# Seven products for eight in the gate and up projections of a fused attention and FFN layer, with down weights loaded at the end

## The chip, the cores and the metric

One Trainium2 chip, all 8 cores, each running the same program on other data. The metric is the time of one execution in device microseconds, which is that of the slowest core. On every core TensorE (PE) does the matrix products, VectorE (DVE), ScalarE (ACT) and GpSimd (POOL) work on elements, and SyncE (SP), ACT and POOL issue DMA transfers.

## What is computed

For four sequences of 4096 tokens of width 1024:

```
s = LN(x) W_spin^T + b;  g = mean(s) W_global;  e = s W_J
x1 = x + LN(tanh(beta * (s + g + softmax(e s^T / 32) s)))
y  = LN(x1);  gate = y w_gate^T / 127;  up = y w_up^T / 127
out = x1 + LN((silu(gate) * up) w_down^T / 127)
```

The hidden width is 3072. The three FFN weights come as int32 between -127 and 127.

## The kernel before

Core c holds sequence c // 2. It projects all 4096 tokens of it, and does the rest for its own 2048 tokens: 16 tiles of 128, or 4 blocks of 512. Matmul operands are bf16, and each matmul is 128x128 by 128x512 into one of the 8 banks of PSUM (`ps`). Each engine has a program of its own (`pe_prog`, `act_prog`, `vec_prog`, `pool_prog`, `sync_prog`), written in the order in which it runs, and waits on semaphores by hand. The stages are:

1. `PHASE_A` (L403 to L448): s and e.
2. `scores` and `values` (L450 to L498) for the 16 token tiles, with softmax, tanh and both layer norms on DVE and ACT. SP transposes each normalised tile `xn2` by DMA into `xn2T` (L292).
3. Gate and up (L500 to L520). The hidden dimension has 24 tiles of 128 (`HC`). A unit is one hidden tile by one block of 512 tokens: 8 matmuls over the 8 slices of the width for gate (L510) and 8 for up (L517). `UNITS` (L45) lists the 96 units. Gate goes to bank n % 4, up to bank 4 + n % 4, so a bank comes round every fourth unit. ACT turns the gate bank into silu in `silu_b` (L620), and DVE multiplies it by the up bank into `h_act` (`h_mul`, L835 to L843).
4. Down (L522 to L543). For each token tile, 24 matmuls into each of two banks, then the last layer norm and the residual: DVE L887 to L914, ACT L628 to L640. SP loads the rows of x1 again (`x1_load`, L296), the first four of them when the last unit is done.

POOL issues the weight loads (L363 to L389). They turn int32 into bf16 on the way, 256 KB landed per tile of gate or of up. The down weights come as six loads of 1 MB (L387) between those of gate and up, and TensorE waits for all six at L522. At the start of stage 3 DVE still has the layer norms of the last token tile to do, so the first products of `h_mul` stand between them:

```python
            h_mul(0)
            ln2_stats(u)
            h_mul(1)
            ln2_apply(u)
            for n in range(2, N_UNIT):
                h_mul(n)
```

## Time and profile before

| What | Value |
|---|---|
| median of 3 runs | 1144.13 us (1143.34 to 1144.13) |
| the profiled execution, its time | 1143.46 us |
| its span on the slowest core, core 2 | 1141.9 us (other cores 1140.5 to 1141.8) |
| TensorE busy | 1116.8 us, 98%, 5200 matmuls |
| DVE, ACT, POOL busy | 446.7, 260.2 and 97.4 us |
| granted TensorE clock | 0.999 on all cores |
| gate and up / down on TensorE | 637.5 to 969.0 us / 969.0 to 1134.8 us |

The span runs from the first to the last instruction of a core; the time of the execution is 1.56 us longer. Times in rows are microseconds from the start of the span unless marked ns. "PEld" is TensorE loading weights, and L510 is line 510 of the kernel.

### The profile page before, as it was taken

What the parts mean: (1) busy time and instruction counts of PE and PEld (TensorE: products, weight loads), DVE (VectorE), ACT (ScalarE), POOL (GpSimd) and SP (SyncE); (2) the same over time, 40 slices, a digit from 0 to 9 for tenths busy, and PEclk for the clock granted to TensorE, in tenths of its full rate; (3) what the DMA queues carried; (4) which work ended last, traced back from release to release, by engine and by line L of the source; (5) the groups of instructions that cost most, each with busy time, mean ns of one, the idle gap of its engine ahead of it and who ended that gap; (6) DMA issues with size and microseconds to landing.
All of it is one profiled execution on the core that took longest, in us unless ns stands there. A gap on an engine that the chain in (4) does not pass through costs nothing.

```text
span 1141.9 us, 15173 instructions; the slowest of 8 cores (1140.5 to 1141.9 us)
## 1 busy us (share of the span) xinstructions
PE 1116.8 (98%) x5200; PEld 508.2 (45%) x5200; DVE 446.7 (39%) x1145; ACT 260.2 (23%) x458; POOL 97.4 (9%) x130
## 2 busy tenths in 40 slices
PE   3999999999999999999999999999999999999997
PEld 2444444444444444444444444444444444444443
DVE  5277600345555555555555721211121122233233
ACT  4434443312222222222222111111111111111111
POOL 4000001001111111111111111111110000000000
PEclk9999999999999999999999999999999999999999
DMA  9988798624433434343333534445542220432321
GB/s 201 205 183 208 165 180 158 106 53 88 89 88 88 86 84 97 94 90 88 90 85 84 105 62 75 74 74 74 74 75 38 37 38 1 148 94 92 111 92 55
DMA packets 172219, 112.15 MB, mean 98 GB/s; under 512 B 146416, under 2 KB 148464, under 8 KB 172144
## 3 DMA queue, kind: packets, MB, share of 16 engines
q1 hardware_dynamic: 151680, 64.77, 25.1%
q0 software_dynamic: 19168, 41.95, 19.7%
q10 hardware_dynamic: 1296, 4.46, 1.2%
q8 instruction: 43, 0.70, 0.3%
q14 instruction: 32, 0.26, 0.1%
HBM read 83.89 MB, written 16.78 MB: 88 GB/s over the span
## 4 chain that ended last, share of the span: by engine, by line
PE 97%; DMA 1%; DVE 0%; issue 0%; ACT 0%; ACTq 0%; DVEq 0%
PE ps L480 19%; PE ps L461 19%; PE ps L510 15%; PE ps L539 15%; PE ps L517 15%; PE ps L445 13%; PE ps L432 2%; DMA xs<-x 1%; PE ps L491 0%; PE ps L396 0%; DVE st L690 0%; ACT xnT L556 0%; ACTq L548 0%; DVE st L691 0%; ACT ob L636 0%
## 5 line engine op out<-in xcount | busy, mean ns | idle before, releaser
L461 PE MATMUL ps<-s_FM,eT 128*128 128x512 bf16 x1024 | 223.6, 379 | 0.0
L480 PE MATMUL ps<-s_tok,pT 128*128 128x512 bf16 x1024 | 223.5, 379 | 0.0
L517 PE MATMUL ps<-xn2T,wgu 128*128 128x512 bf16 x768 | 181.4, 379 | 0.0
L510 PE MATMUL ps<-xn2T,wgu 128*128 128x512 bf16 x768 | 181.4, 379 | 0.0
L539 PE MATMUL ps<-wdT_sb,h_act 128*128 128x512 bf16 x768 | 165.9, 379 | 0.0
L839 DVE SCALAR_TENSOR_TENSOR h_act<-silu_b,ps 128x512 bf16<-128x512 f32 x96 | 65.9, 687 | 251.0 <-PE ps L517 250.5
L480 PEld LDWEIGHTS ps<-s_tok,pT 128*128 128x128 bf16 x1024 | 100.3, 98 | 120.7
L461 PEld LDWEIGHTS ps<-s_FM,eT 128*128 128x128 bf16 x1024 | 100.1, 98 | 120.9
L607 ACT ACTIVATE S_sb<-S_sb,nmx 128x1024 bf16<-128x1024 f32 x64 | 72.7, 1136 | 215.8 <-DVE nmx L773 215.8
L620 ACT ACTIVATE silu_b<-ps 128x512 f32<-128x512 f32 x96 | 57.2, 597 | 268.5 <-PE ps L510 257.8
L539 PEld LDWEIGHTS ps<-wdT_sb,h_act 128*128 128x128 bf16 x768 | 75.1, 98 | 90.6
L517 PEld LDWEIGHTS ps<-xn2T,wgu 128*128 128x128 bf16 x768 | 75.1, 98 | 90.6
L510 PEld LDWEIGHTS ps<-xn2T,wgu 128*128 128x128 bf16 x768 | 75.1, 98 | 90.7 <-issue 0.3
L764 DVE TENSOR_SCALAR_CACHE_REDUCE S_sb<-ps 128x1024 f32<-128x1024 f32 x64 | 78.3, 1223 | 71.5 <-PE ps L461 67.8
L445 PE MATMUL ps<-xnT,wspT_sb 128*128 128x512 bf16 x448 | 97.3, 379 | 0.0
L445 PEld LDWEIGHTS ps<-xnT,wspT_sb 128*128 128x128 bf16 x448 | 43.8, 98 | 52.9
L586 ACT ACTIVATE s_FM<-ps,b_col_sb 128x512 bf16<-128x512 f32 x64 | 43.8, 687 | 58.3 <-PE ps L445 51.0
L791 DVE SCALAR_TENSOR_TENSOR sg<-ps,rinv,sg 128x1024 f32<-128x1024 f32 x16 | 20.5, 1283 | 80.8 <-PE ps L480 80.8
L445 PE MATMUL ps<-s_FM,wjT_sb 128*128 128x512 bf16 x224 | 48.8, 379 | 0.0
L357 POOL TENSOR_TENSOR sg<-s_tok,g_bc 128x1024 f32<-128x1024 bf16 x16 | 34.2, 2134 | 169.0 <-ACT a_bf L602 141.0
L602 ACT ACTIVATE a_bf<-sg,beta_sb 128x1024 bf16<-128x1024 f32 x16 | 18.4, 1147 | 123.9 <-DVE sg L791 123.9
L889 DVE BATCH_NORM_STATS2 st<-ps 128x6 f32<-128x512 f32 x16 | 11.2, 699 | 71.7 <-PE ps L539 71.7
(82 smaller groups left out, 515.6 us busy)
## 6 DMA issues: line engine op xcount, KB each, us to landing
xs<-x SPq DMA_DIRECT2D x24, 512.0 KB, 5.8
xr<-x POOLq DMA_DIRECT2D x16, 512.0 KB, 5.4
x_sc<-xr POOLq DMA_DIRECT2D x16, 512.0 KB, 3.0
x1b<-x_sc SPq DMA_DIRECT2D x16, 512.0 KB, 3.8
out<-ob SPq DMA_DIRECT2D x15, 512.0 KB, 3.8
wgu<-wg POOLq DMA_DIRECT2D x24, 256.0 KB, 4.9
wgu<-wu POOLq DMA_DIRECT2D x24, 256.0 KB, 5.8
wdT_sb<-wdT POOLq DMA_DIRECT2D x6, 1024.0 KB, 12.5
```

Of the source, the lines that this page charges most:

```text
L357: gp.tensor_tensor(out=sg[:], in0=s_tok[:, t - 1, :], in1=g_bc[:], op=ALU.add).then_inc(l_sg, 1)
L445: mm = pe.matmul(bank(b0 + c), w[:, i, o:o + P], moving(i), start=(i == 0), stop=(i == KC - 1))
L461: mm = pe.matmul(bank(2 * slot + half), eT[:, j, t * P:(t + 1) * P], s_FM[:, j, m0:m0 + 512], start=(j == 0), stop=(j == KC - 1))
L480: mm = pe.matmul(bank(pv_bank(t) + nb), pT[:, m, :], s_tok[:, m, nb * 512:(nb + 1) * 512], start=(m == 0), stop=(m == NT - 1))
L510: mm = pe.matmul(bank(n % 4), wgu[:, hb % 3, 0, j, :], xn2T[:, j, tb * 512:(tb + 1) * 512], start=(j == 0), stop=(j == KC - 1))
L517: mm = pe.matmul(bank(4 + n % 4), wgu[:, hb % 3, 1, j, :], xn2T[:, j, tb * 512:(tb + 1) * 512], start=(j == 0), stop=(j == KC - 1))
L539: mm = pe.matmul(bank(2 * slot + nb), h_act[:, c, t * P:(t + 1) * P], wdT[:, c, nb * 512:(nb + 1) * 512], start=(c == 0), stop=(c == HC - 1))
L586: s.activation(out=s_FM[:, c, b * 512:(b + 1) * 512], in_=src, func=AF.Identity, bias=b_col[:, c:c + 1], scale=1.0, accum_out=racc[:, c * ...
L607: s.activation(out=p_view(q), in_=S_sb[:, q, :], func=AF.Exp, bias=nmx[:, t % 2:t % 2 + 1], scale=1.0, accum_out=rs[:, 4 * (t % 2) + q: 4 ...
L620: s.activation(out=silu_b[:, n % 2, :], in_=bank(n % 4), func=AF.Silu).then_inc(a_silu, 1)
L764: v.tensor_scalar(out=S_sb[:, q, :], in0=bank2(2 * (n % 3)), scalar1=INV32, scalar2=None, op0=ALU.mult, op1=ALU.max, accum_out=mx[:, 4 * ( ...
L839: v.scalar_tensor_tensor(out=h_act[:, hb, tb * 512:(tb + 1) * 512], in0=silu_b[:, n % 2, :], scalar=INV127, in1=bank(4 + n % 4), op0=ALU.m ...
```

## The change

**Gate and up.** The first pair of hidden tiles is done as before, in 8 units; of the four token blocks, each is now done for both tiles in turn. The other 11 pairs are done by Strassen's scheme. A step is one pair by two blocks (`STEPS`, 22 of them; q is 0 for token blocks 0 and 1, 1 for blocks 2 and 3). For gate the weights form a 2x2 matrix A (rows: the two hidden tiles, columns: the two halves of the width), and the tokens a matrix B (rows: halves of the width, columns: the two blocks). The plain product needs eight products of such parts for gate, each of 4 matmuls, and Strassen's needs seven, M1 to M7; up is the same. That is 56 matmuls in a step where there were 64. `PRODUCTS` is their order: (m, 0) is product m of gate, (m, 1) of up.

**Sums of inputs.** B11+B22, B11+B12 and B21+B22 go to `u_x`, and B21-B11 and B12-B22 take the place of B21 and B12 in `xn2T`: five DVE additions (`x_sum`) of 128x2048 bf16 for each half of the tokens, between and after the `h_mul` of the first pair. For each pair of weights POOL makes A11+A22, A12-A22 and A21-A11 (`weight_sum`), and DVE -(A21+A22) and -(A11+A12) (`weight_sums`), each 128x1024 bf16 and each for gate and up together.

**Sums of outputs.** A step has two banks for gate and two for up, here z and w. M1 is made in z, and ACT copies it to w, from PSUM to PSUM (L808, L819). M4, -M5 and M7 are then added in z, M3, -M2 and M6 in w, and the banks end as C11 and C22. On the way ACT copies M1, M1+M4 and M1+M3 to SBUF (`t_m1`, `t_14`, `t_13`); POOL makes M4 and M1+M3+M4 of them (L493, L498); and DVE subtracts the bank from that, before M7 and M6 may be added: C12 in `t_14`, C21 in `t_13` (L1157, L1162). ACT takes silu of the four gate blocks, DVE multiplies by up (`hidden`). Steps alternate between two sets of four banks.

**Down weights.** Each of the 24 hidden tiles has its own tile `wdT[c]` and its own load of 256 KB. Six are issued in step (3, 1), seven at the start of step (11, 0), and the last eleven at the start of step (11, 1), the last one. Token tiles 0 and 1 of the down stage are done together, hidden tile by hidden tile, each waiting for its own load.

In the diff, `a_cp`, `a_sl` count ACT's copies and silus, `v_c`, `v_hs`, `v_u`, `v_ws` DVE's subtractions, hidden products and sums, `l_e`, `l_ws` POOL's, and `p_m` TensorE's products.

```diff
-UNITS = ([(0, 0), (0, 1), (0, 2), (1, 0), (1, 1), (1, 2), (0, 3), (1, 3)]
-         + [(hb, tb) for hb in range(2, HC) for tb in range(4)])
...
+UNITS = [(0, 0), (1, 0), (0, 1), (1, 1), (0, 2), (1, 2), (0, 3), (1, 3)]
...
+STEPS = [(p_, q_) for p_ in range(1, NPAIR) for q_ in range(2)]
...
+PRODUCTS = [(1, 0), (1, 1), (4, 0), (3, 0), (4, 1), (3, 1), (5, 0), (2, 0),
+            (5, 1), (2, 1), (7, 0), (6, 0), (7, 1), (6, 1)]
...
+        wd_home = ([192 + 2 * i for i in range(6)]
+                   + [56 + 2 * i for i in range(7)]
+                   + [2 * i for i in range(8)]
+                   + [32 + 2 * i for i in range(3)])
+        wdT = [at(f"wdT{c}", [P, D], BF16, wd_home[c] * KB)
+               for c in range(HC)]
+        WD_EARLY, WD_MID = 6, 13
...
+        def w_operand(s_, gu, m):
+            raw, ext = wraw[s_], wsum[s_]
+            return {1: ext[:, gu, 0, :], 2: ext[:, gu, 1, :],
+                    3: raw[:, gu, 0, 0:512], 4: raw[:, gu, 1, 512:1024],
+                    5: ext[:, gu, 2, :], 6: raw[:, gu, 1, 0:512],
+                    7: raw[:, gu, 0, 512:1024]}[m]
+        def x_operand(q, m):
+            xt, u = xn2T[q], u_x[q]
+            return {1: u[:, 0], 2: xt[:, 0:4, 0:512], 3: xt[:, 0:4, 512:1024],
+                    4: xt[:, 4:8, 0:512], 5: xt[:, 4:8, 512:1024],
+                    6: u[:, 1], 7: u[:, 2]}[m]
+        def step_bank(it, gu, w):
+            return 4 * (it % 2) + 2 * gu + w
...
+            def load_pair(p_):
+                s_ = p_ % 2
+                for i in range(2):
+                    for gu, w_d in enumerate((wg_d, wu_d)):
+                        gp.dma_start(
+                            out=wraw[s_][:, gu, i, :].rearrange(
+                                "p (k f) -> p k f", f=P),
+                            in_=w_d[2 * p_ + i]).then_inc(d_gu[s_][i], 16)
...
+            def weight_sum(p_, i):
+                s_ = p_ % 2
+                raw, ext = wraw[s_], wsum[s_]
+                a11, a12 = raw[:, :, 0, 0:512], raw[:, :, 0, 512:1024]
+                a21, a22 = raw[:, :, 1, 0:512], raw[:, :, 1, 512:1024]
+                if i == 0:
+                    for h in range(2):
+                        gp.wait_ge(d_gu[s_][h], 32 * (p_ // 2 + 1))
+                    gp.tensor_tensor(out=ext[:, :, 0, :], in0=a11, in1=a22,
+                                     op=ALU.add).then_inc(l_ws, 1)
+                    return
+                gp.wait_ge(v_ws, 2 * p_)
+                out, sub = ((a12, a22), (a21, a11))[i - 1]
+                gp.tensor_tensor(out=out, in0=out, in1=sub, op=ALU.subtract
+                                 ).then_inc(l_ws, 1)
...
+                if (p_, q) == (NPAIR - 1, 0):
+                    gp.wait_ge(p_m, NP * it)
+                    for c in range(WD_EARLY, WD_MID):
+                        load_wd(c)
+                if (p_, q) == (NPAIR - 1, 1):
+                    gp.wait_ge(p_m, NP * it)
+                    for c in range(WD_MID, HC):
+                        load_wd(c)
+                for gu in range(2):
+                    gp.wait_ge(a_cp, 8 * it + 5 + 2 * gu)
+                    gp.tensor_tensor(out=t_14[gu][:], in0=t_14[gu][:],
+                                     in1=t_m1[gu][:], op=ALU.subtract
+                                     ).then_inc(l_e, 1)
+                    gp.wait_ge(a_cp, 8 * it + 6 + 2 * gu)
+                    gp.wait_ge(l_e, 4 * it + 2 * gu + 1)
+                    gp.tensor_tensor(out=t_13[gu][:], in0=t_13[gu][:],
+                                     in1=t_14[gu][:], op=ALU.add
+                                     ).then_inc(l_e, 1)
+                if nxt < NPAIR and q == 0:
+                    weight_sum(nxt, 0)
+                elif nxt < NPAIR:
+                    weight_sum(nxt, 1)
+                    weight_sum(nxt, 2)
...
+            for it, (p_, q) in enumerate(STEPS):
+                s_ = p_ % 2
+                for m, gu in PRODUCTS:
+                    if m == 1 and gu == 0:
+                        for h in range(2):
...
+                    elif m == 4:
+                        pe.wait_ge(a_cp, 8 * it + 1 + 2 * gu)
+                    elif m == 3:
+                        pe.wait_ge(a_cp, 8 * it + 2 + 2 * gu)
+                    elif m == 5:
+                        pe.wait_ge(a_cp, 8 * it + 5 + 2 * gu)
+                        pe.wait_ge(v_ws, 2 * p_)
+                    elif m == 2:
+                        pe.wait_ge(a_cp, 8 * it + 6 + 2 * gu)
+                    elif m == 7:
+                        pe.wait_ge(v_c, 4 * it + 1 + 2 * gu)
+                        pe.wait_ge(l_ws, 3 * p_ - 1)
+                    else:
+                        pe.wait_ge(v_c, 4 * it + 2 + 2 * gu)
...
+            pe.wait_ge(v_h, N_UNIT)
+            pe.wait_ge(a_sl, 4 * (N_STEP - 1))
+            pe.wait_ge(v_hs, 4 * (N_STEP - 1))
+            for c in range(HC):
+                pe.wait_ge(d_wd[c], 16)
+                for t in range(2):
+                    for nb in range(2):
+                        mm = down(t, nb, c)
+                        if c == HC - 1:
+                            mm.then_inc(p_dn, 1)
+            for t in range(2, NQ):
+                if t == 2:
+                    pe.wait_ge(a_sl, 4 * N_STEP)
+                    pe.wait_ge(v_hs, 4 * N_STEP)
+                elif t >= 4:
...
+                n0 = 8 * it
+                zg, wg_, zu, wu_ = [bank(step_bank(it, gu, w))
+                                    for gu in range(2) for w in range(2)]
+                s.wait_ge(p_m, product_done(it, 1, 0))
+                if it == 1:
+                    s.wait_ge(v_h, N_UNIT)
+                s.copy(out=wg_, in_=zg).then_inc(a_cp, 1)
+                s.wait_ge(a_cp, n0 + 1)
+                if it == 0:
+                    s.wait_ge(v_h, N_UNIT)
+                else:
+                    s.wait_ge(v_hs, 4 * it - 1)
+                s.copy(out=t_m1[0][:], in_=wg_).then_inc(a_cp, 1)
+                s.wait_ge(p_m, product_done(it, 1, 1))
+                if it >= 2:
+                    s.wait_ge(v_hs, 4 * (it - 1))
+                s.copy(out=wu_, in_=zu).then_inc(a_cp, 1)
+                s.wait_ge(a_cp, n0 + 3)
+                if it >= 1:
+                    s.wait_ge(v_hs, 4 * it)
+                s.copy(out=t_m1[1][:], in_=wu_).then_inc(a_cp, 1)
+                for gu, (z, w) in enumerate(((zg, wg_), (zu, wu_))):
+                    s.wait_ge(p_m, product_done(it, 4, gu))
+                    s.copy(out=t_14[gu][:], in_=z).then_inc(a_cp, 1)
+                    s.wait_ge(p_m, product_done(it, 3, gu))
+                    s.copy(out=t_13[gu][:], in_=w).then_inc(a_cp, 1)
+                for i, t_ in enumerate((t_14[0], t_13[0])):
+                    s.wait_ge(v_c, 4 * it + i + 1)
+                    s.activation(out=t_[:], in_=t_[:], func=AF.Silu
+                                 ).then_inc(a_sl, 1)
+                for i, (t_, z, m) in enumerate(((t_m1[0], zg, 7),
+                                                (t_m1[1], wg_, 6))):
+                    s.wait_ge(p_m, product_done(it, m, 0))
+                    s.wait_ge(l_e, 4 * it + 2 * i + 1)
+                    s.activation(out=t_[:], in_=z, func=AF.Silu
...
+                b11, b12 = xt[:, 0:4, 0:512], xt[:, 0:4, 512:1024]
+                b21, b22 = xt[:, 4:8, 0:512], xt[:, 4:8, 512:1024]
+                v.wait_ge(d_xn2T, 16 * (8 * q + 8))
+                if i >= 3:
+                    v.wait_ge(p_up, 4 * q + 4)
+                out, in0, in1, op = ((u_[:, 0], b11, b22, ALU.add),
+                                     (u_[:, 1], b11, b12, ALU.add),
+                                     (u_[:, 2], b21, b22, ALU.add),
+                                     (b21, b21, b11, ALU.subtract),
+                                     (b12, b12, b22, ALU.subtract))[i]
+                v.tensor_tensor(out=out, in0=in0, in1=in1, op=op
+                                ).then_inc(v_u, 1)
+            def weight_sums(p_):
+                s_ = p_ % 2
+                for h in range(2):
+                    v.wait_ge(d_gu[s_][h], 32 * (p_ // 2 + 1))
+                for i, h in ((1, 1), (2, 0)):
+                    v.scalar_tensor_tensor(
+                        out=wsum[s_][:, :, i, :],
+                        in0=wraw[s_][:, :, h, 0:512], scalar=-1.0,
+                        in1=wraw[s_][:, :, h, 512:1024],
+                        op0=ALU.mult, op1=ALU.subtract).then_inc(v_ws, 1)
+            v.wait_ge(p_qk, 4 * NQ)
+            h_mul(2)
+            x_sum(0, 0)
+            h_mul(3)
+            x_sum(0, 1)
+            h_mul(4)
+            x_sum(0, 2)
+            weight_sums(1)
+            h_mul(5)
+            x_sum(0, 3)
+            h_mul(6)
+            x_sum(0, 4)
+            h_mul(7)
+            v.wait_ge(v_u, 5)
+            for i in range(5):
+                x_sum(1, i)
...
+            for it, (p_, q) in enumerate(STEPS):
+                for gu in range(2):
+                    v.wait_ge(l_e, 4 * it + 2 * gu + 2)
+                    v.wait_ge(p_m, product_done(it, 5, gu))
+                    v.tensor_tensor(out=t_14[gu][:], in0=t_13[gu][:],
+                                    in1=bank(step_bank(it, gu, 0)),
+                                    op=ALU.subtract).then_inc(v_c, 1)
+                    v.wait_ge(p_m, product_done(it, 2, gu))
+                    v.wait_ge(v_c, 4 * it + 2 * gu + 1)
+                    v.tensor_tensor(out=t_13[gu][:], in0=t_13[gu][:],
+                                    in1=bank(step_bank(it, gu, 1)),
+                                    op=ALU.subtract).then_inc(v_c, 1)
+                v.wait_ge(v_c, 4 * it + 4)
+                v.wait_ge(a_sl, 4 * it + 1)
+                hidden(it, 0, 1, t_14[0][:], t_14[1][:])
+                v.wait_ge(a_sl, 4 * it + 2)
+                hidden(it, 1, 0, t_13[0][:], t_13[1][:])
+                v.wait_ge(a_sl, 4 * it + 3)
+                v.wait_ge(p_m, product_done(it, 7, 1))
+                hidden(it, 0, 0, t_m1[0][:], bank(step_bank(it, 1, 0)))
+                v.wait_ge(a_sl, 4 * it + 4)
+                v.wait_ge(p_m, product_done(it, 6, 1))
+                hidden(it, 1, 1, t_m1[1][:], bank(step_bank(it, 1, 1)))
+                if q == 0 and p_ + 1 < NPAIR:
+                    weight_sums(p_ + 1)
```

What it moves, first on TensorE in the gate and up stage. Before, parts of two units (gate L510, up L517):

```order
L517 MATMUL ps<-xn2T,wgu 128x512 x7
L510 MATMUL ps<-xn2T,wgu 128x512 [waits d_gu1,d_xn2T,a_silu]
L510 MATMUL ps<-xn2T,wgu 128x512 x7
L517 MATMUL ps<-xn2T,wgu 128x512 [waits v_h]
L517 MATMUL ps<-xn2T,wgu 128x512 x7
```

Now, the start of step (2, 0) (`wsum` and `wraw` hold weights, `u_x` and `xn2T` tokens; M1 of gate, M1 of up, M4 of gate):

```order
L682 MATMUL ps<-u_x_66,wsum_70 128x512 [waits d_gu0_0,d_gu0_1,l_ws,a_sl]
L682 MATMUL ps<-u_x_66,wsum_70 128x512 x3
L682 MATMUL ps<-u_x_66,wsum_70 128x512 [waits v_hs]
L682 MATMUL ps<-u_x_66,wsum_70 128x512 x3
L686 MATMUL ps<-xn2T_45,wraw_68 128x512 [waits a_cp]
L686 MATMUL ps<-xn2T_45,wraw_68 128x512 x3
```

A wait now stands before every fourth matmul, and M4 of gate (the fifth row) waits for a copy that ACT makes of M1 of gate, with one product in between. M3 of gate, M4 and M3 of up follow with such waits too.

Next DVE, from the last layer norm on (`xn` is `xn2`). Before:

```order
L680 SCALAR_TENSOR_TENSOR nw<-nw 128x1 [waits v_seq]
L830 TENSOR_SCALAR xn_62<-xr,mv,nw 128x1024 [waits v_seq,d_xn2T]
L839 SCALAR_TENSOR_TENSOR h_act<-silu_b,ps 128x512 [waits a_silu,p_up] x94
L887 BN_STATS st_73<-ps 128x6 [waits p_dn]
L889 BN_STATS st_73<-ps 128x6 [waits p_dn]
```

Now, to the fourth addition over the first half of the tokens:

```order
L1056 SCALAR_TENSOR_TENSOR h_act<-tmp_72,ps 128x512 [waits p_qk,a_silu,p_up]
L1112 TENSOR_TENSOR u_x_66<-xn2T_45 128x2048 [waits d_xn2T]
L1056 SCALAR_TENSOR_TENSOR h_act<-tmp_73,ps 128x512 [waits a_silu,p_up]
L1112 TENSOR_TENSOR u_x_66<-xn2T_45 128x2048 [waits d_xn2T]
L1056 SCALAR_TENSOR_TENSOR h_act<-tmp_72,ps 128x512 [waits a_silu,p_up]
L1112 TENSOR_TENSOR u_x_66<-xn2T_45 128x2048 [waits d_xn2T]
L1121 SCALAR_TENSOR_TENSOR wsum_71<-wraw_69 128x2x512 [waits d_gu1_0,d_gu1_1]
L1121 SCALAR_TENSOR_TENSOR wsum_71<-wraw_69 128x2x512
L1056 SCALAR_TENSOR_TENSOR h_act<-tmp_73,ps 128x512 [waits a_silu,p_up]
L1112 TENSOR_TENSOR xn2T_45<-xn2T_45 128x4x512 [waits d_xn2T,p_up]
```

Between the products of the first pair stand the sums, here 128x2048 and 128x1024 in size; one more of the first half and five of the second follow.

Last POOL, near the end of its program. Before, at the last of the six loads of down weights:

```order
L381 DMA wgu<-wg 128x1024 [waits p_up]
L383 DMA wgu<-wu 128x1024
L387 DMA wdT_sb<-wdT 128x4x1024
L381 DMA wgu<-wg 128x1024 [waits p_up]
L383 DMA wgu<-wu 128x1024
```

Now, from the seventh load of step (11, 0) into the eleven of step (11, 1):

```order
L422 DMA wdT12_96<-wdT 128x1024
L493 TENSOR_TENSOR tmp2_74<-tmp2_74,tmp0_72 128x512 [waits a_cp]
L498 TENSOR_TENSOR tmp4_76<-tmp4_76,tmp2_74 128x512 [waits a_cp,l_e]
L493 TENSOR_TENSOR tmp3_75<-tmp3_75,tmp1_73 128x512 [waits a_cp]
L498 TENSOR_TENSOR tmp5_77<-tmp5_77,tmp3_75 128x512 [waits a_cp,l_e]
L422 DMA wdT13_97<-wdT 128x1024 [waits p_m]
L422 DMA wdT14_98<-wdT 128x1024
```

The additions that the banks wait for (L493, L498) now stand behind weight loads on the queue of POOL. The load of wdT6 to wdT12 comes ahead of the first row, that of the other ten of the last step behind the last.

## Rows read from the trace of the kernel before

**Rows 1.** The page: engines' busy time; all cores; shares of the chain.
```profile
PE 1116.8 (98%) x5200; PEld 508.2 (45%) x5200; DVE 446.7 (39%) x1145; ACT 260.2 (23%) x458; POOL 97.4 (9%) x130
...
PE 97%; DMA 1%; DVE 0%; issue 0%; ACT 0%; ACTq 0%; DVEq 0%
...
core 2: 1141.9 us, clock 0.999
```

**Rows 2.** Stretches: length, busy us (instructions) of PE, PEld, DVE, ACT, POOL, clock, DMA share, GB/s.
```profile
0.00:30.00 30.00, 11.84 (x82) 7.62 (x83) 16.26 (x45) 14.99 (x22) 12.55 (x24) 1.00 0.94 198
...
637.48:969.04 331.56, 331.56 (x1538) 150.21 (x1537) 75.99 (x132) 59.63 (x98) 27.36 (x49) 1.00 0.38 60
```

**Rows 3.** Groups by line: shapes and count, busy us, mean ns, idle before and its releasers.
```profile
L839 DVE SCALAR_TENSOR_TENSOR h_act<-silu_b,ps 128x512 bf16<-128x512 f32 x96 | 65.9, 687 | 251.0 <-PE ps L517 250.5 <-ACT silu_b L620 0.3 <-DVE mv L801 0.2
L620 ACT ACTIVATE silu_b<-ps 128x512 f32<-128x512 f32 x96 | 57.2, 597 | 268.5 <-PE ps L510 257.8 <-DVE h_act L839 10.7
L586 ACT ACTIVATE s_FM<-ps,b_col_sb 128x512 bf16<-128x512 f32 x64 | 43.8, 687 | 58.3 <-PE ps L445 51.0 <-PE ps L432 7.3
L357 POOL TENSOR_TENSOR sg<-s_tok,g_bc 128x1024 f32<-128x1024 bf16 x16 | 34.2, 2134 | 169.0 <-ACT a_bf L602 141.0 <-DVE g_bc L866 28.0
L812 DVE SCALAR_TENSOR_TENSOR xr<-a_bf,nw,xr 128x1024 f32<-128x1024 bf16 x16 | 20.6, 1285 | 2.9 <-DVE nw L680 2.9
L674 DVE TENSOR_TENSOR nw<-nw 128x1 f32<-128x1 f32 x96 | 15.3, 159 | 10.6 <-DVE nw L669 0.6 <-DVE nw L680 0.3
L754 DVE TENSOR_SCALAR mf_bc<-mf 128x1024 bf16<-128x1024 f32 x1 | 0.7, 693 | 0.1
L921 DVE TENSOR_TENSOR ob<-ob,x1b 128x512 f32<-128x512 f32 x1 | 0.7, 693 | 0.3 <-ACT ob L636 0.3
```

**Rows 4.** Timeline, the last unit of gate and up: start us, length us, instruction.
```profile
965.58 1.89 PE L510 MATMUL ps<-xn2T,wgu 128*128 128x512 bf16 x8
967.31 1.89 PE L517 MATMUL ps<-xn2T,wgu 128*128 128x512 bf16 x8
967.62 0.60 ACT L620 ACTIVATE silu_b<-ps 128x512 f32<-128x512 f32 x1 [2.86 <-PE ps L510]
969.04 21.32 PE L539 MATMUL ps<-wdT_sb,h_act 128*128 128x512 bf16 x98
969.31 0.69 DVE L839 SCALAR_TENSOR_TENSOR h_act<-silu_b,ps 128x512 bf16<-128x512 f32 x1 [2.77 <-PE ps L517]
```

**Rows 5.** Timeline, start of the kernel: DVE waits for itself, TensorE for ACT.
```profile
9.23 0.14 DVE L699 RECIPROCAL ri<-sd 128x1 f32<-128x1 f32 x1
...
9.48 0.16 DVE L701 SCALAR_TENSOR_TENSOR nb<-mv,ri 128x1 f32<-128x1 f32 x1
...
12.29 1.24 ACT L572 ACTIVATE xn<-xs,nb,ri 128x1024 bf16<-128x1024 f32 x1
...
13.64 0.78 PEld L396 LDWEIGHTS ps<-ident,xn 128*128 128x128 bf16 x8 [2.38 <-issue]
13.67 1.01 PE L396 MATMUL ps<-ident,xn 128*128 128x128 bf16 x8 [2.15 <-ACT xn L572]
```

**Rows 6.** Timeline of DVE, the end of the last layer norm.
```profile
654.02 0.81 DVE L830 TENSOR_SCALAR xn<-xr,mv,nw 128x1024 bf16<-128x1024 f32 x1 [0.18 <-DVE nw L680]
654.75 1.28 DVE L839 SCALAR_TENSOR_TENSOR h_act<-silu_b,ps 128x512 bf16<-128x512 f32 x2
```

**Rows 7.** Timeline of POOL: issues of one gate tile and of 1 MB of down weights.
```profile
721.11 0.53 POOL L381 DMA_DIRECT2D wgu<-wg  x1 [12.75 <-PE ps L517]
...
722.15 0.78 POOL L387 DMA_DIRECT2D wdT_sb<-wdT  x1
```

**Rows 8.** DMA from issue to landing: gate tile; down weights; x1b.
```profile
wgu<-wg POOLq DMA_DIRECT2D x24, 256.0 KB, 4.9
...
DMA to landing us min/median/max: 11.9/12.5/13.2
...
DMA to landing us min/median/max: 3.6/3.8/9.6
```

197 lines of the change are left out of this document (128 added, 69 removed).

## Prediction

> **What bounds the kernel now.** I read the page and the cores first. All cores end together at a granted clock of 1.00, the fuller of TensorE's two levels (2.4 GHz), and 97% of the chain that ended last is TensorE [rows 1]. So work taken off TensorE shortens the kernel, as far as nobody else becomes late. The stretches give TensorE's pace: gate and up last 331.56 us for 96 units of 16 matmuls (the row counts two at its edges besides), 215.9 ns each, busy all through [rows 2]. DVE is busy for 76 us of it, ACT for 60, POOL for 27. The groups give prices, and say that ACT and DVE spend their idle time there waiting for TensorE [rows 3]. What decides is how quickly results go round, so I read handoffs last, in timelines [rows 4, 5]. ACT starts 0.31 us after TensorE's next group has started (967.31 to 967.62), DVE 0.27 us after (969.04 to 969.31). From ACT's end (13.53) to TensorE's next matmul (13.67) it is 0.14 us. A DVE instruction that waits for DVE's last one starts 0.11 us behind its end (9.37 to 9.48); I take that for ACT, POOL and any pair of them too.
>
> **Removed from TensorE.** 22 steps x 8 matmuls = 176, at 215.9 ns: **-38.0 us**. 5024 are left. A product then lasts 4 x 0.2159 = 0.863 us, a step of 14 products 12.09 us. The pace itself stays: a wait that has been met costs nothing where the units have theirs (1536 matmuls fill the stage without a gap).
>
> **One step, followed through.** Times from its start, at which M1 of gate starts. M1 of gate is followed at 0.86, ACT starts its copy to bank w at 1.17, and ends at 1.77, with 0.60 as for L620 [rows 3]. M4 of gate can start at 1.91, and its place is 1.73: **0.18 us late**, in each of 22 steps, **+4.0 us**. No row shows ACT writing to PSUM. Below, I take 0.50 a copy (0.1 us less than any, 0.08 late, 1.8 us in all); above, the 0.687 of L586 (0.27 late, 5.9 us).
> The other copies have time: the second (1.88 to 2.48) frees M3 of gate, placed at 2.77 with the 0.18; the fifth, M1+M4 of gate, ends at 4.35, and M5 is placed at 5.36.
> POOL then adds four times, with one wait for itself in each pair. L357 takes 2.134 us for 1024 elements, so 1.07 for 512 [rows 3]. From 4.46: 5.53, then 5.64 to 6.71, to 7.78, and 7.89 to 8.96. DVE subtracts with 0.69 (L921): the third ends at 9.76, the fourth, which waits for it, at 10.56. M7 of up is placed at 10.54 and could start at 9.90; M6 of up at 11.40, and could at 10.70. So 0.64 us are spare in POOL's four additions: up to 1.23 us each they cost nothing. That is the narrowest cover of the change.
> In a step ACT has 12 x 0.6 = 7.2 us of work, DVE 8 x 0.69 and up to 2 x 1.29 of weight sums (L812), 8.1, POOL 4.3 and up to 4.3 of weight sums: all below 12.3. POOL's two sums of an odd step end at 8.96 + 2 x 2.13 + 0.11 = 13.3, 1.1 us into the next step; four loads at 0.53 [rows 7] end at 3.2, before it is needed at 4.46. Nothing on the path.
>
> **Start of the steps.** DVE's queue is behind here. Its last layer norm lets it go at 654.75 [rows 6], and TensorE needs the five sums of the first half after its 8 units, at 637.48 + 128 x 0.2159 = 665.11 [rows 2]. Before them stand five products at 0.64 and two weight sums at 1.285 (L812), 5.8 us. The price of a sum of 2048 bf16 elements is in no row. L754, the one DVE row with dense bf16 written and no second tensor, takes 0.693 us for 1024; less the 0.16 us of a single element (L674) this is 0.52 ns per element, 1.23 us for 2048. L921, TENSOR_TENSOR on 32-bit words, gives (0.693 - 0.16)/512 = 1.04 ns, 2.29 us. I take 1.23, because all three tensors are 16 bits wide here, as in L754's output. The sums end at 654.75 + 5.8 + 6.2 = 666.7, and the first step starts 1.7 us late: **+1.7 us**. The five sums of the second half end at 673.5, and M7 needs DVE at 674.5: hidden. With 2.29 the first step is 7.0 us late, DVE comes free 4.0 us late for M7, and the sum is 11.0 us.
> "VectorE: DVE Perf Modes" of the Trainium skill (section on the perf-mode tier table) has tensor_tensor on 2048 bf16 elements at 1224 ns, and 2293 ns on fp32; the second agrees with L921, the first is in no row.
>
> **Down weights.** In step (11, 0) POOL issues seven loads of 256 KB from 1.1 on: at 0.53 each, as a gate tile of the same size [rows 7], to 4.8, so its additions start 0.3 late, covered. In step (11, 1) eleven last from 0.1 to 6.0, its additions start 1.6 late, and 0.64 is spare: **+1.0 us**. At the 0.78 us of L387 it is 1.5 + 3.6 = 5.1 us, the upper end.
> Arrival: the gate tile issued at 721.11 lands after 4.9 us, at 726.0; the tile of up and the 1 MB behind it are in at 722.15 + 12.5 = 734.65 [rows 7, 8]. That is 1.25 MB in 8.65 us, 1.73 us for 256 KB. The eighteen late loads are then in at 1.1 + 4.9 + 17 x 1.73 = 35.4 from the start of (11, 0). The four x1b loads come among them and took up to 9.6 us [rows 8]: 45.0 at the latest. The last tile is needed at 2 x 12.27 + 1.0 + 92 x 0.2159 = 45.4. No cost, but only just: 10% less bandwidth makes 3 us. The wait for all six big loads at the stage's start (L522) had cost nothing, so nothing is gained. The first two token tiles end together, 20.7 us into the stage, but DVE has until the fifth tile, at 41 us.
>
> **Sum.** 1141.9 - 38.0 + 4.0 + 1.7 + 1.0 = 1110.6 us of span. The profiled execution took 1.56 us more than its span, and the median is 0.67 above that execution: **1112.8 us**. It is 2.7% below 1144.13.
>
> **Rivals.**
> *POOL and DVE get in each other's way.* In odd steps POOL's two weight sums run from 9.0 to 13.3, and DVE's first two hidden products (both factors in SBUF) are due at 10.7. If such a pair can't run together and POOL goes first, DVE starts at 13.3, and its third product, which frees `t_m1` for ACT's second copy, ends 3.1 us into the next step, not 0.8. The copy ends at 3.9, M3 starts at 4.0 instead of 2.8: 1.2 us in 10 steps, 12 us, **1125**. For it: no row has the two together, since L357 ran alone. Against: if DVE gets in between the two sums, it costs 0. 20%.
> "SBUF — State Buffer" of the Trainium skill (section Who interferes with whom) says that a DVE instruction with two SBUF inputs and a GpSimd instruction that reads SBUF can't run at once, and that the later one waits for the whole of the other. No row here shows it; by it alone this rival would be the forecast whenever POOL wins the second turn.
> *DVE's sums take 2.29 us.* +9.3 us, **1122**. 10%.
> *Down weights come too late.* 20% less bandwidth for casting loads beside x1b: 6 to 7 us at the start of down, **1119**. 8%.
> *Slower than before: POOL's additions of f32.* L357 reads one bf16 tensor; here both are 32 bits wide. If that doubles an element, an addition of 512 takes 2.13 us, each step is 4 x (2.13 - 1.23) = 3.6 us late at M7 of up, 22 times 79 us: **1192**. It decides from 1.23 us on, and the gain is gone at 1.23 + 33/88 = 1.6 us. Against: of L357's three tensors two, `g_bc` and `sg`, are 32 bits wide already. 4%.
> *The change doesn't do what it says.* The order of instructions shows the 176 matmuls gone, so it could only be that TensorE runs slower: if the gaps brought its granted clock down from 1.00, each percent over 22 steps would cost 2.7 us. At the kernel's start TensorE was busy for 11.84 of 30 us, and the granted clock was 1.00 [rows 2]. 3%, **1120**.
>
> **Chances.** The forecast as summed has 55%, the rivals 45%. The range from **1108 to 1130** takes in the lower ends (ACT at 0.50, sums hidden) and all rivals but the slow one, but not two of them together. A measurement of this kernel can tell 0.2%, some 2.3 us. Faster by more than that: 0.95, within it 0.01, slower 0.04.
>
> **What would show it.** Right: 5024 matmuls; M4 of gate idle before it by some 0.2 us for ACT L808, and nothing before M3, M5, M2; L493 and L498 near 1.07 us; one wait of 1 to 3 us before the first L682, released by DVE L1112 at 1.2 us each; one wait near 1 us for DVE at M7 of up in the last step; the down stage starting near 638 + 27.6 + 1.7 + 22 x 12.27 + 1 = 938. Wrong: TensorE waiting at M7 or M6 in every step (POOL's price), at M3 in even steps (the two in each other's way), at L693 for a weight load, or L808 longer than 0.7 us.

## The result and the profile after

The changed kernel takes **1136.68 us** (median; 1135.7 to 1137.2), the kernel before 1144.13: a ratio of 0.9936, 95% interval 0.9919 to 0.9953. It is faster, by 7.4 us, where a gain of 31.3 was forecast: 1112.8 us, with a range from 1108 to 1130. So 23.9 us have to be explained. Executions in which a die showed a markedly lower granted clock are left out of all ratios and ranges, here and below; they move the medians given by at most 0.4 us, and e7's, which they would move by 0.9, is given without them.

The profiled execution took 1136.68 us for a span of 1135.1 (core 5; the others 1129.8 to 1134.3, granted clocks 0.995 to 0.999). From the page, to set beside [rows 1]: busy times, the chain that ended last, and the down stage's matmuls (line, engine, tiles, count, busy us and mean ns, idle us before them).

```profile
PE 1089.2 (96%) x5024; PEld 487.4 (43%) x5024; DVE 570.8 (50%) x1265; ACT 357.2 (31%) x634; POOL 292.3 (26%) x269
...
PE 84%; issue 5%; POOL 4%; DVE 3%; ACT 2%; DMA 1%; POOLq 0%; ACTq 0%; DVEq 0%
...
L693 PE MATMUL ps<-wdT,h_act 128*128 128x512 bf16 x768 | 165.9, 379 | 0.0
```

The matmuls are gone, 5024 are left, and those of the down stage run without a gap. But TensorE's share of the chain fell from 97% to 84%, and POOL, DVE and ACT are in it. The waits of TensorE say where (what ended them; us in all, times, longest):

```profile
PE ps L686 <- ACT tmp L814: 9.8, 12, 0.9
PE ps L686 <- DVE tmp L1157: 7.1, 19, 1.5
...
PE ps L682 <- DVE xn2T L1112: 3.6, 1, 3.6
```

L814 is ACT's second copy, for which M3 of gate waits; L1157 the subtraction ahead of M7; L1112 the x sums. The rows are those of core 5, the slowest. The times at which M1 of gate starts (L682) give every step its length; the table has them for core 7, on which no weight load was late (more on that below). The forecast stands beside it:

| | forecast | core 7 |
|---|---|---|
| first step starts at | 666.8 | 668.59 |
| step 0 | 12.27 | 13.93 |
| the ten later steps with q = 0 | 12.27 | 13.6 each |
| the ten steps with q = 1, but the last | 12.27 | 12.4 each |
| the last step | 13.3 | 14.75 |
| down stage starts at | 938 | 957.63 |

On core 5 the down stage starts at 962.24. From there to the end it is 172.9 us on both cores, as in the kernel before (969.04 to 1141.9).

**The steps with q = 0.** Timeline of core 7 round the start of such a step, at 747.04 (start and duration in us, engine, line, tiles; in brackets idle time and what ended it):

```profile
744.16 4.66 POOL L439 TENSOR_TENSOR wraw<-wraw 128x1024 bf16<-128x1024 bf16 x2
...
746.03 3.34 DVE L1146 SCALAR_TENSOR_TENSOR h_act<-tmp,tmp 128x512 bf16<-128x512 f32 x2 [0.17 <-ACT tmp L837]
...
747.04 1.89 PE L682 MATMUL ps<-u_x,wsum 128*128 128x512 bf16 x8
...
749.29 1.27 DVE L1146 SCALAR_TENSOR_TENSOR h_act<-tmp,ps 128x512 bf16<-128x512 f32 x2
...
750.06 0.59 ACT L814 COPY tmp<-ps 128x512 f32<-128x512 f32 x1 [1.32 <-DVE h_act L1146]
...
750.79 2.75 PE L686 MATMUL ps<-xn2T,wraw 128*128 128x512 bf16 x12 [0.89 <-ACT tmp L814]
```

POOL makes the two weight sums of the step before, and beside them DVE's first two hidden products, both factors in SBUF, take 3.34 us, where such a pair takes 1.3 in the last step, with no sum of POOL's beside it. The same view in shorter windows parts the pairs:

```profile
746.25 2.57 POOL L439 TENSOR_TENSOR wraw<-wraw 128x1024 bf16<-128x1024 bf16 x1
...
746.76 2.60 DVE L1146 SCALAR_TENSOR_TENSOR h_act<-tmp,tmp 128x512 bf16<-128x512 f32 x1
```

POOL's first sum runs from 744.16 and takes 2.13 us, as if alone. DVE's first product starts at 746.03 and is over by 746.8; it came in between the two sums. POOL's second sum takes 2.57 us instead of 2.13, and DVE's second product, started inside it, 2.60 instead of 0.68. In the middle of that the new step starts. DVE's third product frees `t_m1` only then; ACT's copy had stood idle for 1.32 us, and M3 of gate for 0.89. TensorE waits so in ten steps.

The groups of core 7 (mean ns of one), to set beside [rows 3], between 600 and 960 us:

```profile
L493 POOL TENSOR_TENSOR tmp<-tmp,tmp 128x512 f32<-128x512 f32 x44 | 56.4, 1282 | 65.6 <-ACT tmp L826 65.6
L498 POOL TENSOR_TENSOR tmp<-tmp,tmp 128x512 f32<-128x512 f32 x44 | 55.8, 1267 | 6.3
L439 POOL TENSOR_TENSOR wraw<-wraw 128x1024 bf16<-128x1024 bf16 x22 | 51.7, 2373 | 11.6 <-DVE wsum L1121 11.6
L1146 DVE SCALAR_TENSOR_TENSOR h_act<-tmp,tmp 128x512 bf16<-128x512 f32 x44 | 50.1, 1177 | 3.8 <-ACT tmp L837 2.9 <-DVE tmp L1162 0.9
...
L1146 DVE SCALAR_TENSOR_TENSOR h_act<-tmp,ps 128x512 bf16<-128x512 f32 x44 | 28.0, 674 | 0.0
...
L1121 DVE SCALAR_TENSOR_TENSOR wsum<-wraw 128x1024 bf16<-128x1024 bf16 x22 | 25.8, 1211 | 0.0
L434 POOL TENSOR_TENSOR wsum<-wraw 128x1024 bf16<-128x1024 bf16 x11 | 23.4, 2126 | 0.0
...
L808 ACT COPY ps<-ps 128x512 f32<-128x512 f32 x22 | 12.6, 571 | 53.7 <-PE ps L682 53.7
```

POOL's additions take 1.27 us, not 1.07. A hidden product with a factor in PSUM takes 0.674 us, each time; one with both factors in SBUF 1.177 on the mean. ACT's copy to PSUM is quick, 0.571, and M4 of gate is 0.1 us late for it, where 0.18 was taken.

**The start of the steps.** The same view, and then windows of core 7 (the stretch, its length, PE busy and matmuls in it, the granted clock, DMA share, GB/s):

```profile
658.34 1.22 DVE L1112 TENSOR_TENSOR u_x<-xn2T 128x2048 bf16<-128x2048 bf16 x1
...
661.97 5.18 POOL L439 TENSOR_TENSOR wraw<-wraw 128x1024 bf16<-128x1024 bf16 x2 [11.62 <-DVE wsum L1121]
662.35 2.83 DVE L1112 TENSOR_TENSOR xn2T<-xn2T 128x2048 bf16<-128x2048 bf16 x1
...
665.70 2.54 DVE L1112 TENSOR_TENSOR xn2T<-xn2T 128x2048 bf16<-128x2048 bf16 x1
...
668.59 1.01 PE L682 MATMUL ps<-u_x,wsum 128*128 128x512 bf16 x2 [3.74 <-DVE xn2T L1112]
```

```profile
668.50:670.00 1.50, 1.41 (x4) 0.50 0.94 107
670.00:672.00 2.00, 2.00 (x7) 0.60 1.07 201
672.00:676.00 4.00, 4.00 (x20) 1.00 0.71 118
```

The first three x sums take 1.22 us each, as forecast. The last two meet POOL's L439 and take 2.83 and 2.54, and POOL's pair 5.18 instead of 4.3. TensorE stands still for 3.74 us. Then, which is in no term of the sum, the granted clock is 0.50 and 0.60: for most of these 3.5 us it is the lower of the two levels, 1.2 GHz. Eight matmuls last 3.36 us instead of 1.89. This does not follow on every core. On cores 1 and 3 the pause is as long (3.63 and 3.64 us), the granted clock stays at 1.00, and yet step 0 lasts 13.69 us, only 0.24 less than on core 7. So the lower clock is not what makes step 0 long. Core 1, the first matmuls and POOL's first two additions:

```profile
667.93 1.89 PE L682 MATMUL ps<-u_x,wsum 128*128 128x512 bf16 x8 [3.63 <-DVE xn2T L1112]
...
672.14 1.81 POOL L493 TENSOR_TENSOR tmp<-tmp,tmp 128x512 f32<-128x512 f32 x1 [3.42 <-ACT tmp L826]
...
674.09 2.06 POOL L498 TENSOR_TENSOR tmp<-tmp,tmp 128x512 f32<-128x512 f32 x1
```

The additions take 1.81 and 2.06 us instead of 1.27. DVE makes its last x sums of the second half beside them, until 675.0, and then waits 1.30 us for POOL (L498) before it can subtract; M7 of gate and of up are late in turn.

**The last step.** POOL on core 7:

```profile
943.60 5.87 POOL L422 DMA_DIRECT2D wdT<-wdT  x11 [3.56 <-PE ps L686]
949.39 1.37 POOL L493 TENSOR_TENSOR tmp<-tmp,tmp 128x512 f32<-128x512 f32 x1
...
953.53 1.26 POOL L498 TENSOR_TENSOR tmp<-tmp,tmp 128x512 f32<-128x512 f32 x1
```

The eleven issues end at 949.4, 6.5 us into the step. TensorE waits 1.50 us before M7 of gate and 0.74 before M7 of up.

### The profile page after: what moved, and what is told of

The parts are those of the page before. It is cut to its first block, busy times and chain, and to the rows that moved or that the text cites. A ratio compares the mean times of both kernels' runs of the same rounds, so it can differ in the third digit from the quotient of the medians.

```text
span 1135.1 us, 15989 instructions; the slowest of 8 cores (1129.8 to 1135.1 us)
## 1 busy us (share of the span) xinstructions
PE 1089.2 (96%) x5024; PEld 487.4 (43%) x5024; DVE 570.8 (50%) x1265; ACT 357.2 (31%) x634; POOL 292.3 (26%) x269
## 4 chain that ended last, share of the span: by engine, by line
PE 84%; issue 5%; POOL 4%; DVE 3%; ACT 2%; DMA 1%; POOLq 0%; ACTq 0%; DVEq 0%
PE ps L597 19%; PE ps L578 19%; PE ps L693 15%; PE ps L561 13%; PE ps L686 12%; POOL tmp L493 2%; PE ps L548 2%; DVE h_act L1146 2%; PE ps L628 1%; PE ps L636 1%; POOL tmp L498 1%; DMA xs<-x 1%; POOL wdT L422 1%; PE ps L682 1%; ACT tmp L814 1%
## 5 line engine op out<-in xcount | busy, mean ns | idle before, releaser
L693 PE MATMUL ps<-wdT,h_act 128*128 128x512 bf16 x768 | 165.9, 379 | 0.0
L784 ACT ACTIVATE S_sb<-S_sb,nmx 128x1024 bf16<-128x1024 f32 x64 | 72.7, 1136 | 215.9 <-DVE nmx L990 215.9
L693 PEld LDWEIGHTS ps<-wdT,h_act 128*128 128x128 bf16 x768 | 75.1, 98 | 90.6
L686 PE MATMUL ps<-xn2T,wraw 128*128 128x512 bf16 x352 | 81.7, 378 | 9.9 <-ACT tmp L814 9.8
L686 PE MATMUL ps<-u_x,wraw 128*128 128x512 bf16 x352 | 83.1, 379 | 7.4 <-DVE tmp L1157 7.1
L1157 DVE TENSOR_TENSOR tmp<-tmp,ps 128x512 f32<-128x512 f32 x44 | 30.3, 688 | 111.8 <-PE ps L686 66.0
L686 PE MATMUL ps<-xn2T,wsum 128*128 128x512 bf16 x352 | 79.6, 379 | 0.0
L493 POOL TENSOR_TENSOR tmp<-tmp,tmp 128x512 f32<-128x512 f32 x44 | 57.8, 1313 | 59.6 <-ACT tmp L826 59.6
L1146 DVE SCALAR_TENSOR_TENSOR h_act<-tmp,tmp 128x512 bf16<-128x512 f32 x44 | 58.8, 1374 | 3.8 <-DVE tmp L1162 2.3
L498 POOL TENSOR_TENSOR tmp<-tmp,tmp 128x512 f32<-128x512 f32 x44 | 55.7, 1267 | 6.3
L686 PEld LDWEIGHTS ps<-xn2T,wraw 128*128 128x128 bf16 x352 | 32.0, 97 | 58.8 <-issue 26.9
```

The costliest lines, as they stand in the source:

```text
L493: gp.tensor_tensor(out=t_14[gu][:], in0=t_14[gu][:], in1=t_m1[gu][:], op=ALU.subtract).then_inc(l_e, 1)
L498: gp.tensor_tensor(out=t_13[gu][:], in0=t_13[gu][:], in1=t_14[gu][:], op=ALU.add).then_inc(l_e, 1)
L686: mm = pe.matmul(dst, w[:, j * P:(j + 1) * P], xo[:, j, :], start=False, stop=(j == 3), skip_group_check=True)
L693: return pe.matmul(bank(2 * (t % 4) + nb), h_act[:, c, t * P:(t + 1) * P], wdT[c][:, nb * 512:(nb + 1) * 512], start=(c == 0), stop=(c == ...
L784: s.activation(out=p_view(q), in_=S_sb[:, q, :], func=AF.Exp, bias=nmx[:, t % 2:t % 2 + 1], scale=1.0, accum_out=rs[:, 4 * (t % 2) + q: 4 ...
L1146: v.scalar_tensor_tensor(out=h_act[:, 2 * p_ + h, (2 * q + tb) * 512:(2 * q + tb + 1) * 512], in0=gate, scalar=INV127, in1=up, op0=ALU.mul ...
```

## The experiments

The experiments are e1 to e12 in the order of this section. Ratios are to the kernel before, run on the same chip; "step" is the distance from one M1 of gate to the next. The theory at this point: POOL and an instruction of DVE that reads two tensors from SBUF keep each other waiting (A, most often); its rivals are plain bandwidth, DVE's own queue, and late DMA.

### DVE's products in another order

```diff
-                hidden(it, 0, 1, t_14[0][:], t_14[1][:])
-                hidden(it, 1, 0, t_13[0][:], t_13[1][:])
...
                 hidden(it, 0, 0, t_m1[0][:], bank(step_bank(it, 1, 0)))
...
                 hidden(it, 1, 1, t_m1[1][:], bank(step_bank(it, 1, 1)))
+                hidden(it, 0, 1, t_14[0][:], t_14[1][:])
+                hidden(it, 1, 0, t_13[0][:], t_13[1][:])
```

> Base: the changed kernel. DVE makes the two hidden products that have a factor in PSUM first, and the two with both factors in SBUF (t_14, t_13) last; ACT and TensorE wait for the renumbered products. Theory A (a DVE instruction with two SBUF inputs and POOL's two weight sums of an odd step can't run together; the products with a PSUM factor can): the products tmp,ps take 0.68 us each beside POOL's L439, t_m1 is free for ACT's second copy before the next step needs it, the 0.89 us wait of M3 of gate is gone in all ten steps that have it. A step with q=0 goes from 13.6 to about 12.5 us, the time from 1136.7 to about 1126 us. Theory B (POOL's sums slow down whatever DVE does, by sharing bandwidth to SBUF): the products tmp,ps take 1 us or more as well, M3 still waits 0.5 us or more, and the time falls by less than 6 us.

**1124.31 us** (0.9828, interval 0.9814 to 0.9842). Theory A. M3's wait is gone in all ten steps with q = 0, and nine of them last 12.41 to 12.45 us on core 7. The tenth, (11, 0), still lasts 13.30: there POOL issues seven down loads ahead of its additions until 4.97 us into the step, where the additions of the others start at 4.27, and M7 of up waits 0.85 us. In the changed kernel that was out of sight behind M3's wait (13.67 against 13.6). The timeline of core 7 shows why the nine are short:

```profile
741.69 4.22 POOL L439 TENSOR_TENSOR wraw<-wraw 128x1024 bf16<-128x1024 bf16 x2
...
743.99 0.69 DVE L1150 SCALAR_TENSOR_TENSOR h_act<-tmp,ps 128x512 bf16<-128x512 f32 x1 [0.59 <-PE ps L686]
...
744.85 0.69 DVE L1150 SCALAR_TENSOR_TENSOR h_act<-tmp,ps 128x512 bf16<-128x512 f32 x1 [0.17 <-PE ps L686]
745.46 1.00 DVE L1150 SCALAR_TENSOR_TENSOR h_act<-tmp,tmp 128x512 bf16<-128x512 f32 x1
```

POOL's same two sums run from 741.69 to 745.91. Inside that DVE's two products with a PSUM factor take 0.69 us each, as ever; the next, from SBUF alone, started while POOL's second sum ran, takes 1.00. DVE's work is the same in amount; only its order changed. A bandwidth that all of DVE's instructions share with POOL would have stretched the PSUM ones as well.

### Without POOL's two differences

```diff
-                gp.tensor_tensor(out=out, in0=out, in1=sub, op=ALU.subtract
-                                 ).then_inc(l_ws, 1)
+                gp.wait_ge(l_ws, 3 * (p_ - 1) + i)
+                gp.memset(nw[:, 11:12], 0.0).then_inc(l_ws, 1)
```

> Base: the changed kernel. Left out: POOL's two weight sums A12-A22 and A21-A11 of each pair (one column is set to zero in their place), so M6 and M7 work with wrong weights; all else is there and the loads have the same waits. Theory A (they keep DVE waiting wherever it reads two tensors from SBUF): L1146 with both factors in SBUF takes 1.3 to 1.4 us a pair everywhere, not 3.3; M3's 0.89 us wait is gone in ten steps (10.5 us); the x sums at the start of the steps take 1.22 us each, not 2.83 and 2.54, and the first step starts about 2.9 us earlier. Sum: 1136.7 - 10.5 - 2.9 = about 1123 us. Theory B (the x sums are slow for a reason of their own, such as the queue of DVE or the transposes' DMA): x sums of 2.5 us and more stay, and the time is 1126 or more.

**1123.27 us** (0.982, 0.9806 to 0.9834). Theory A on the x sums: 1.22 us each, and the first step starts at 665.5 on core 7, 3.1 us sooner. The granted clock stays at 1.00, but step 0 lasts 14.03 us: POOL's first addition, now beside the last x sums, takes 2.94 us.

```profile
662.32 1.22 DVE L1112 TENSOR_TENSOR xn2T<-xn2T 128x2048 bf16<-128x2048 bf16 x1
...
664.05 1.22 DVE L1112 TENSOR_TENSOR xn2T<-xn2T 128x2048 bf16<-128x2048 bf16 x1
```

But Theory A's products of 1.3 to 1.4 us a pair everywhere did not come: those from SBUF still took 952 ns each on the mean on core 7, not 675, and some steps with q = 1 lasted 13.0 to 13.7. POOL's remaining sum, L434, had waited 10.1 us in all, nine times, for its weights' DMA on core 7; on core 1, where it never did, the span was 1116.5 us and not 1122.0. The same stands in the changed kernel: on core 5 L434 waits 8.4 us (nine times) and the steps with q = 1 last up to 13.68; on core 7 it never waits and they last 12.42. A later run takes this up.

### Without the fourth addition

```diff
+                    if gu == 0:
                         gp.tensor_tensor(out=t_13[gu][:], in0=t_13[gu][:],
                                          in1=t_14[gu][:], op=ALU.add
                                          ).then_inc(l_e, 1)
+                    else:
+                        gp.memset(nw[:, 11:12], 0.0).then_inc(l_e, 1)
```

> Base: the changed kernel. Left out: POOL's fourth addition of a step, M1+M3+M4 of up (one column is set to zero in its place), so the lower left quarter of up is wrong. Theory A (POOL's four additions at 1.26 us are a chain that ends too late for DVE's fourth subtraction, and M7 of up waits for it): the wait of 0.21 to 0.4 us before M7 of up is gone in every step, a q=1 step lasts 12.2 us, and the time is about 22 x 0.25 = 5.5 us less, and 1 us less in the last step: 1130 us. Theory B (M7 of up waits for DVE's own queue, not for POOL): the wait stays, the time falls by less than 2 us.

**1119.28 us** (0.9784, 0.977 to 0.9798). M7's wait is gone and a step with q = 1 lasts 12.19 us on core 7: Theory A. But 17.4 us went where 6.5 were expected. The steps with q = 0 fell from 13.6 to 12.32 on core 7 (to as much as 12.9 on others): POOL's weight sums begin 8.4 us into the step instead of 9.5 when one addition is gone. DVE's pair is stretched as before (3.40 us), but it starts sooner and ends 1.4 us into the next step instead of 2.3. The price of POOL's chain and the two in each other's way are not separate terms.

### What an addition of POOL takes

```diff
+    for k, (a, b, n) in enumerate(
+            ((qa, qb, 256), (qa, qb, 512), (qa, qb, 1024),
+             (ha, hb_, 256), (ha, hb_, 512), (ha, hb_, 1024))):
+        gp.tensor_tensor(out=a[:, 0:n], in0=a[:, 0:n],
+                         in1=b[:, 0:n], op=ALU.add
+                         ).then_inc(l_q, 1)
```

> Base: the kernel before. Added on POOL in the gate and up stage, at four tiles: six additions in a row, each waiting for the last, of 256, 512 and 1024 elements, with two f32 inputs and f32 output, then the same with bf16 throughout. Theory A (an addition has a fixed part, so that half of the price of 1024 elements was too little for 512): f32 at 512 elements takes 1.26 us with nobody beside it, as in the changed kernel, 256 about 0.85 and 1024 about 2.1; bf16 the same within 5%. Theory B (1.26 us is stretched by DVE and ACT working beside it in the changed kernel): here 512 takes 1.07 us, half of 1024. Nothing waits for these additions; the time of the kernel stays 1144 or rises slightly where a weight load is issued later.

1143.79 us in the profiled execution. Groups of POOL:

```profile
L400 POOL TENSOR_TENSOR xr<-xr 128x1024 f32<-128x1024 f32 x4 | 9.4, 2349 | 0.6
L400 POOL TENSOR_TENSOR xr<-xr 128x1024 bf16<-128x1024 bf16 x4 | 8.5, 2118 | 0.6
L400 POOL TENSOR_TENSOR xr<-xr 128x512 f32<-128x512 f32 x4 | 5.1, 1265 | 0.6
...
L400 POOL TENSOR_TENSOR xr<-xr 128x512 bf16<-128x512 bf16 x4 | 4.6, 1150 | 0.6
L400 POOL TENSOR_TENSOR xr<-xr 128x256 f32<-128x256 f32 x4 | 3.0, 754 | 0.0
L400 POOL TENSOR_TENSOR xr<-xr 128x256 bf16<-128x256 bf16 x4 | 2.7, 667 | 0.6
```

Theory A: 1.265 us, as in the changed kernel, with nothing of DVE's that reads two tensors from SBUF beside it. From 256 to 512 elements an f32 addition grows by 511 ns, from 512 to 1024 by 1084, so 0.18 to 0.24 us of it do not grow with the length; with bf16 it is 0.18. Three of its numbers missed: 256 elements were put at 0.85 us (0.754), 1024 at 2.1 (2.349), and bf16 within 5% of f32, which is 10 to 13% dearer.

### The x sums earlier

```diff
+                if t == NQ:
+                    v.wait_ge(p_qk, 4 * NQ)
+                    for i in range(3):
+                        x_sum(0, i)
                 if u >= 0:
                     field(u)
```

> Base: the changed kernel. DVE makes the first three x sums before its last row of layer norm, as soon as the transposed tokens are there and the last scores have been read, not between the hidden products. Theory A (the first step started 3.6 us late because the x sums ran at 2.8 and 2.5 us beside POOL's two weight sums, at the end of DVE's queue): at the new place an x sum takes 1.22 us and nobody waits for it; the wait before the first product falls to 0 to 1 us, step 0 from 14.0 to about 12.5, since the sums that it needs are ready; together 4 to 5 us: about 1132 us. Theory B (DVE's queue is the bound in this stretch, so the three sums only push the layer norm and the transposed last row back by 3.7 us, and TensorE waits there instead): the first step starts no earlier, and the time stays at 1135 to 1138 us.

**1132.48 us** (0.9899, 0.9882 to 0.9917), 4.2 less. TensorE waits 0.6 us ahead of the first product, and its first eight matmuls last 1.89 us again; on core 7 the first step starts 3.2 us sooner. Half of the reason was wrong. The two sums beside L439 still take 2.84 and 2.55 us; they are only early enough now. And step 0 still takes 13.69 us on core 7, where 12.5 was expected, as on cores 1 and 3 of the changed kernel: POOL's first two additions take 1.80 and 2.06 us beside the last sums of the second half, and DVE then waits 1.29 us for POOL. On most cores of the changed kernel the lower clock had hidden this wait and cost little beyond it.

### The down loads of the last step split

```diff
-                    for c in range(WD_MID, HC):
+                    for c in range(WD_MID, WD_MID + 7):
...
+                if (p_, q) == (NPAIR - 1, 1):
+                    for c in range(WD_MID + 7, HC):
+                        load_wd(c)
```

> Base: the changed kernel. In the last step POOL issues seven of the eleven down weight loads before its additions and four after them. Theory A (the last step's 14.7 us, its waits of 1.5 and 0.74 us at M7, come from the eleven issues at 0.53 us ahead of the additions): the additions start 2.1 us earlier, the step lasts about 12.6 us, and the time falls by about 2.0 us, to 1134.7. Theory B (the loads that are issued 5 us later come too late for the down products): the same stands at the start of the down stage as a wait at L693, and nothing is gained.

**1133.78 us** (0.9913, 0.9897 to 0.9929), 2.9 less, where 2.0 was expected. Theory A. The trace accounts for 2.1: the last step takes 12.66 us on core 1, against 14.76, and L693 has no wait, though the last four tiles are asked for 5.3 us later in the step (9.8 us into it, against 4.5).

### DVE makes the fourth addition

```diff
+                    if gu == 1:
+                        v.wait_ge(l_e, 3 * it + 3)
+                        v.wait_ge(a_cp, 8 * it + 8)
+                        v.tensor_tensor(out=t_13[1][:], in0=t_13[1][:],
+                                        in1=t_14[1][:], op=ALU.add
+                                        ).then_inc(v_a, 1)
```

> Base: the kernel with DVE's hidden products reordered (e1_order, 1124.3 us). POOL's fourth addition of a step, M1+M3+M4 of up, is made by DVE, and POOL's weight sums wait for it. Theory A (after e1 what keeps M7 of up waiting by 0.2 us in each step is the length of POOL's chain of four at 1.27 us): DVE's addition takes 0.7 us (two f32 inputs in SBUF, with nothing of POOL's beside it), M7 of up is no longer late, a step lasts 12.2 us, and the time is 22 x 0.23 = 5 us below e1's, near 1119. Theory B (DVE's own chain of three is as long as POOL's last addition was): M7 of up waits as before, 1124.

**1123.9 us** (0.9826, 0.981 to 0.9842), hardly a gain over e1's 1124.31, but not for Theory B's reason. On cores 0 to 3 Theory A holds: spans of 1114.0 to 1117.9 us, where e1 had 1119.1 to 1122.4, and on core 0 the steps from the fourth to the twentieth last 12.18 or 12.19 us. On cores 4 to 7 TensorE is slow. On core 4 it is busy for every one of the 240 us from 680 to 920, and gets through fewer matmuls than on core 3 (core 4 first):

```profile
680.00:800.00 120.00, 120.00 (x542) 0.98 0.34 53
800.00:920.00 120.00, 120.00 (x539) 0.97 0.25 41
```

```profile
680.00:800.00 120.00, 119.96 (x551) 1.00 0.34 57
800.00:920.00 120.00, 120.00 (x553) 1.00 0.24 41
```

The granted clock is 0.97 to 0.98, and what the waits had cost stands in the matmuls.

### All together

The edits of e7, e5 and e6 in one, and in step (11, 0):

```diff
-                    for c in range(WD_EARLY, WD_MID):
+                    for c in range(WD_EARLY, WD_EARLY + 3):
```

> Base: e7_dve_adds with the early x sums of e5 and the split down weight loads of e6; in the step before the last, three of the seven down loads ahead of POOL's additions and four behind them. Theory A (the four causes, the two in each other's way, POOL's price, the x sums and the issues, are separate and add up): 1119 - 4 - 2 - 0.8 = about 1112 us, the time that the prediction had; steps of 12.2 us throughout. Theory B (taking one away lets the next one show): 1116 us or more, with a wait at a new place.

**1118.28 us** (0.9778, 0.9763 to 0.9794). The time is Theory B's, not Theory A's 1112. On cores 0 to 3 spans of 1107.5 to 1110.8, and steps of 12.19 us, 17 of the 22 on core 3, as Theory A has it; on cores 4 to 7 a clock of 0.97 to 0.98 from 680 to 920 us, and spans of 1111.7 to 1115.8. There is no wait at a new place, but POOL and DVE still meet. On core 0 POOL's remaining first sum (here L435) waits 3.80 us for a load and runs from 752.38 beside DVE's pair from SBUF, which takes 2.18 us; DVE's own weight sums come late by that and stretch POOL's next addition to 2.19 us; M7 waits, and the step lasts 13.30 us.

### Without any sum of POOL

The edit of e2, and for L434:

```diff
+                    if p_ > 2:
+                        gp.wait_ge(l_ws, 3 * (p_ - 1))
+                        gp.memset(nw[:, 11:12], 0.0).then_inc(l_ws, 1)
+                        return
                     gp.tensor_tensor(out=ext[:, :, 0, :], in0=a11, in1=a22,
```

> Base: the changed kernel. Left out: all weight sums of POOL (of A11+A22 the ones from the third pair on, and A12-A22 and A21-A11 of every pair), with one column set to zero in place of each; M1, M6 and M7 work with wrong weights. e2 left out two of the three, and some steps with q=1 still lasted 13.0 to 13.7 us. Theory A (those are the steps in which POOL's remaining sum, L434, waited for its weights' DMA and so ran beside DVE's hidden products of the step before): with L434 gone too, L1146 with both factors in SBUF takes 0.65 to 0.7 us each everywhere, every step lasts 12.4 us on every core, and the time is 2 to 3 us below e2's 1123.3. Theory B (it is the DMA itself that delays TensorE or DVE, through d_gu): some steps still last 13 us, DVE waiting for the DMA before its own weight sums, and the time is as e2's.

**1118.75 us** (0.9778, 0.9765 to 0.9792), 4.5 below e2, more than expected. Theory A: the steps from the second to the twentieth take 12.4 to 12.5 us, on core 0 and on core 7, and a product from SBUF takes 691 ns on the mean:

```profile
L1150 DVE SCALAR_TENSOR_TENSOR h_act<-tmp,tmp 128x512 bf16<-128x512 f32 x44 | 28.6, 691 | 3.8 <-ACT tmp L841 3.3 <-DVE tmp L1166 0.5
```

So in these steps the DMA delays TensorE only by way of POOL: a load that is late moves L434 to where DVE's products are. Steps 0 (13.93 us on core 7), (11, 0) (12.77) and the last (14.77), which have other causes, stay long, so "every step 12.4" did not come.

### The addition left to POOL, and two kernels over again

e10 is e8 without this; e11 is e8, e12 the changed kernel:

```diff
-                        v.tensor_tensor(out=t_13[1][:], in0=t_13[1][:],
-                                        in1=t_14[1][:], op=ALU.add
-                                        ).then_inc(v_a, 1)
```

> Base: e8_together, but POOL keeps the fourth addition (so the order of DVE's products, the early x sums and the split down loads are there). Theory A (e8 missed 1112 because the granted clock falls to 0.97 on one die once TensorE is busy without a gap and the gaps of 0.24 us a step are of use to it): here the steps last 12.43 us, the clock in the steps is 0.99 to 1.00 on both dies, and the time is 1117 us, the same as e8's within 1 us. Theory B (the clock has nothing to do with the gap at M7): the clock in the steps is 0.97 on that die again, the gap is paid besides, and the time is 1121 us or more.

> e8_together once more, unchanged, beside e10 and e12 on the same chip. Theory A (the lower clock belongs to this kernel's steps): one die or both show 0.96 to 0.98 in the steps again, and the time is 1118 us. Theory B (it belonged to the chip of the last runs): the clock is 0.998 on both dies, and the time is 1111 to 1112 us.

> The changed kernel itself, as a control on the same chip as e9 to e11. 1136.7 us, with steps of 13.6 and 12.4 to 13.7 us and a clock of 0.995 to 0.999. If this chip gave a lower clock to any kernel with these steps (against theory A of e11), it would show here as well.

On one chip: **1118.17 us** with the addition on POOL (0.9777, 0.9764 to 0.9791), **1113.66** with it on DVE (0.9738, 0.9724 to 0.9751), and the changed kernel 1135.91. The fourth addition's place is worth 4.5 us, near the 5 expected. e10's time is near its Theory A's, but it spoke against it: the clock falls with the gaps of 0.24 us in place as well. Core 0, e10 and then e11:

```profile
740.00:752.00 12.00, 11.95 (x46) 0.81 0.82 119
752.00:764.00 12.00, 12.00 (x55) 0.95 0.03 5
```

```profile
740.00:752.00 12.00, 12.00 (x47) 0.81 0.80 132
752.00:764.00 12.00, 12.00 (x55) 0.96 0.02 4
```

The granted clock is 0.81 over the same 12 us in both, between the two levels, after 12 us in which TensorE had been busy for 11.7 of them and more at 0.99 to 1.00; one step takes 14.3 to 14.4 us. From 680 to 800 us the clock was 0.98 on cores 0 and 1 in e10 and on cores 0 to 3 in e11, and 1.00 on the others. It is not in every execution: the profiled one of e11 took 1116.4 us, the other three, with mean clocks of 0.998 and 0.999 on all cores, 1112.4 to 1113.8, near what its Theory B expects. Nor does it take steps without gaps: in the trace of e6, whose steps before the last are those of the changed kernel, cores 4 to 7 show 0.81 from 744 to 748 us, and in that of e5 cores 4 and 5 show 0.81 from 742 to 745. The changed kernel in its two traces shows nothing of it. What brings it about stays open: no run took it away by itself. The same kernel took 1113.7 us here and 1118.3 as e8, on another chip. On the die with the full clock the two agree: spans of 1107.4 to 1110.5 here, 1107.5 to 1110.8 there. So the difference is the clock.

## Why the prediction was wrong

The step that failed is the overlap of the helpers. The sum let POOL and DVE work side by side at the prices that each has alone, and it put their standing in each other's way at nothing, as a rival with a chance of 20%. Two terms around it were too small besides: POOL's addition and the start of the steps.

**The pace and the sum's big term held.** 176 matmuls at 215.9 ns: the shortest step of the last runs, 12.19 us, is the 12.09 of fourteen products and 0.10 for M4.

**"Rivals: POOL and DVE get in each other's way", at 20%, is what happened.** It was put at 1.2 us in ten steps, 12 us in all, and that price was right. Measured: steps of 13.5 to 13.8 us in each of the ten, on every core, against 12.4 without it. M3 has 1.05 of it on core 7 (its place is 2.69 us into the step, it starts 3.75 into it). The argument against it, that it costs 0 if DVE gets in between the two sums, fell short: DVE did get in between, with its first product; the second met POOL's second sum and took 2.60 us. The argument had thought of one product where there are two. "SBUF — State Buffer" of the Trainium skill (Who interferes with whom) had this rule, and e1, e2 and e9 agree with it: 0.69 us with a factor in PSUM beside POOL's sums, 1.0 and more without where the two meet, and 0.69 on the mean when POOL's sums are gone. By that rule alone the rival would have been the forecast.

**"Start of the steps": the price was right, the company was left out.** The x sum takes 1.22 us alone, as taken. But the rival was thought through for the hidden products only. Two of the sums fell on POOL's L439, and 1.7 us of delay became 3.6 to 3.7. "M7 needs DVE at 674.5: hidden" failed too: the sums of the second half were done in time for DVE, but POOL's additions were stretched beside them, and step 0 lasts at least 13.69 us instead of 12.27. The lower clock behind the pause slowed eight matmuls by 1.5 us; against cores 1 and 3, which did not have it, it lengthened step 0 by 0.2 to 0.4 us on five cores and by 1.3 on core 4, since M7 would have waited anyway. e5 gave 4.2 us back, and step 0's wait is not in that.

**"That is the narrowest cover of the change", 1.07 us an addition with cover up to 1.23, was the mis-sized term.** Half of 2.134 us leaves the fixed part out; it is 1.265. That is 0.04 us an addition over the cover, 0.14 us in all by the prediction's terms; M7 of up is late by 0.23 us in steps with q = 1 and by 0.36 in those with q = 0. So a step lasts 12.42 us on core 7 where e7 has 12.19, and it is 4.5 us from e10 to e11. The longer chain also pushed POOL's weight sums back, from 8.96 us into the step to 9.54, onto DVE's products.

**"Down weights": the arrival was right, the delay too small.** No wait at L693. The last step was to lose 1.0 us for eleven issues at 0.53. The issues took 0.53 each (5.87 us), but the dearer additions had no 0.64 us to spare, and M7 of gate waits as well: 14.75 us instead of the 12.42 of other steps, 2.3, of which e6's trace has 2.1 back. The seven issues of (11, 0), "covered", were not either: with M3's wait gone, e1 shows 0.9 us for them, and e8, which splits them, has that step at 12.19 us.

**Late weights on some cores** are a cause that the prediction did not have. Why the loads come late on some cores and not on others stays open. A step with q = 1 is up to 1.26 us longer where L434 starts late. It made core 5 some 4 us slower than core 7, and the time is that of the slowest core.

**ACT's copies to PSUM** cost less than taken: 0.10 instead of 0.18 us, 1.8 us in all.

**Together**, in the changed kernel's own trace: on core 7 the start is 1.8 us later than forecast, step 0 1.7 longer, the ten later steps with q = 0 13.4, those with q = 1 1.6, and the last 1.5, some 20 us; core 5 starts its down stage 4.6 us after core 7. That is the 23.9.

By the experiments, the products' order gave 12.4 us, the x sums 4.2, the down loads 2.9 and the fourth addition 4.5, 24.0 in all; all at once gave 23.0 (1136.7 to 1113.7), or 22.3 against the changed kernel on the same chip (1135.9). The times of e1, e5 and e6 come from other chips, and by the intervals of the ratios each difference is uncertain by some 2 us.

That 1113.7 is so near the forecast of 1112.8 is luck. The new kernel no longer has what the sum still charged for the start (1.7, now 0.6), for the loads (1.0) and for M4 (4.0, in fact 2.2); by the sum's terms it would take about 1109 us, an estimate. Instead it has step 0 at 13.3 us, steps with q = 1 of up to 13.4 us after late loads on six of the cores, and in some executions the lower clock.

## What to carry to other kernels

When work moves off TensorE to helpers, follow each helper's instruction to its neighbours in time on the others, and look for an interference at all places where the pair can meet, not only at the one where it was first seen: here there were four, and either of the two was the one held up. Read as many operands from PSUM as the data's place allows, or order the instructions so that those with two SBUF tensors are the ones that nobody waits for: moving two products behind two others gave 12 us here. An experiment that takes one wait away may show a second one behind it, as step (11, 0) did. Price a short instruction from two lengths, never by halving a long one.

## What had not been expected of the hardware

- A POOL addition and a DVE instruction with two tensors in SBUF stretch each other. POOL's sum of 128x1024 bf16 went from 2.13 us to 2.57 and 3.10, its f32 addition of 512 elements from 1.27 to as much as 2.94; DVE's x sum from 1.22 to 2.83, its product from 0.68 to 2.61. A product with a factor in PSUM is not touched (0.69).
- After a pause of 3.74 us TensorE's granted clock on core 7 was 0.50 and 0.60 for 3.5 us, and 1.00 again behind it. On cores 1 and 3, after pauses of 3.6 us, it was 1.00 throughout. After the pause of 0.6 us in e5 the first eight matmuls ran at the full pace.
- A granted clock of 0.81 for 3 to 12 us, and of 0.97 to 0.98 on the mean of 240 us, came on cores of one die only: the short falls in e5, e6, e10 and e11, with and without gaps in the steps, the long stretches in e7 and e8. The kernel before, which has no gap at all in the same place, showed 1.00 on all its cores.
- An f32 addition on POOL takes 0.754, 1.265 and 2.349 us for 256, 512 and 1024 elements.
